# Another order of the statements on the four compute engines of a six-layer transformer pipeline

## The reference

```python
for i in range(DEPTH):                       # 6
    x = attn_layer(shift_tokens(x), Wqkv[i], q_scale[i], k_scale[i], Wo[i]) + x
    x = ffn_layer(shift_tokens(x), ln_g[i], ln_b[i], W1[i], b1[i], W2[i], b2[i]) + x
```

## Time and profile before

| | us |
|---|---|
| median of 3 runs | 3971.73 (3968.78 to 3972.18) |
| the profiled execution: its time | 3966.87 |
| its span | 3965.1 |
| PE busy | 3589.4 (91%) |
| PE's weight loads busy | 2946.9 (74%) |
| DVE busy | 3022.7 (76%) |
| ACT busy | 2842.0 (72%) |
| POOL busy | 2308.3 (58%) |
| share of PE in the chain that ended last | 67% |

### The profile page before, as it was taken

One profiled execution on the slowest core, in us unless ns is written; L12 is line 12 of the kernel. 1 busy time (PEld: TensorE's weight loads), 2 busy tenths in 40 slices (PEclk: granted clock), 3 DMA queues, 4 the chain that ended last, 5 costly groups with the idle time before them and its releaser, 6 DMA issues.

```text
span 3965.1 us, 140581 instructions
## 1 busy us (share of the span) xinstructions
PE 3589.4 (91%) x58802; PEld 2946.9 (74%) x58802; DVE 3022.7 (76%) x5808; ACT 2842.0 (72%) x5375; POOL 2308.3 (58%) x2139
## 2 busy tenths in 40 slices
PE   4755645999999999999999999999999999999998
PEld 3634433788878888878888888888788887888886
DVE  4577767877787777887777877777877778877774
ACT  2322214888888888888888888888888888878886
POOL 1000004767666667766677666776667766666762
PEclk9777756999999999999999999999999999999999
DMA  2000002433333333344333333333333333343332
GB/s 63 24 30 12 2 13 63 114 93 88 90 88 105 105 89 88 94 105 111 91 87 88 94 100 105 90 92 93 105 106 89 88 94 93 95 108 98 102 98 55
DMA packets 149461, 331.94 MB, mean 84 GB/s; under 512 B 17632, under 2 KB 27616, under 8 KB 147168
## 3 DMA queue, kind: packets, MB, share of 16 engines
q1 hardware_dynamic: 148832, 322.93, 30.7%
HBM read 218.01 MB, written 104.86 MB: 81 GB/s over the span
## 4 chain that ended last, share of the span: by engine, by line
PE 67%; DVE 7%; ACT 6%; issue 4%; POOL 0%; DVEq 0%; ACTq 0%; POOLq 0%
PE bank L1670 19%; PE bank L1729 9%; PE bank L1787 8%; PE bank L1760 7%; PE bank L1707 7%; PE bank L1744 4%; PE bank L1837 3%; PE bank L1775 3%; ACT L1328 3%; PE bank L1828 3%; DVE rot_a L1470 2%; DVE rot_b L1477 2%; DVE ss L1485 2%; ACT pT L1262 1%; ACT gate L1328 1%
## 5 line engine op out<-in xcount | busy, mean ns | idle before, releaser
L1131 POOL TENSOR_TENSOR qk<-rot_a,rot_b 128x512 f32<-128x512 f32 x768 | 985.8, 1284 | 763.0 <-PE bank L1707 746.4
L1141 POOL TENSOR_TENSOR qk<-qk,rn 128x512 f32<-128x512 f32 x768 | 798.9, 1046 | 144.2 <-DVE rn L1549 144.2
L1470 DVE TENSOR_TENSOR rot_a<-bank,rot 128x512 f32<-128x512 f32 x768 | 528.9, 689 | 265.3 <-PE bank L1670 256.9
L1213 ACT ACTIVATE sq<-bank 128x512 f32<-128x512 f32 x768 | 461.5, 601 | 223.1 <-DVE rot_b L1477 165.8
L1670 PE MATMUL bank<-w_hi,xs_hi 128*128 128x512 f32 x1152 | 583.1, 506 | 35.4 <-POOL xs_lo L1121 18.2
L1485 DVE TENSOR_REDUCE ss<-sq 128x8 f32<-128x512 f32 x768 | 515.6, 671 | 46.3 <-ACT sq L1213 46.1
L1477 DVE TENSOR_TENSOR rot_b<-bank,rot 128x512 f32<-128x512 f32 x768 | 522.1, 680 | 0.0
L1707 PE MATMUL bank<-ident,qk 128*128 128x128 f32 x3072 | 471.1, 276 | 4.7 <-ACT qT L1224 1.9
L1670 PE MATMUL bank<-w_lo,xs_hi 128*128 128x512 f32 x1152 | 458.2, 398 | 0.0
L1670 PE MATMUL bank<-w_hi,xs_lo 128*128 128x512 f32 x1152 | 456.6, 396 | 0.0
L1729 PEld LDWEIGHTS bank<-kT,qT 64*32 64x32 f32 x24576 | 359.9, 107 | 121.1 <-issue 120.9
(11 more groups left out here) (235 smaller groups left out, 6843.8 us busy)
## 6 DMA issues: line engine op xcount, KB each, us to landing
vw<-value_scratch SPq DMA_DIRECT2D x576, 256.0 KB, 4.9
value_scratch<-v SPq DMA_DIRECT2D x192, 512.0 KB, 2.7
vw<-value_scratch SPq DMA_DIRECT2D x192, 192.0 KB, 3.7
stage<-in_wqkv SPq DMA_DIRECT2D x6, 1536.0 KB, 9.3
stage<-in_wb_all SPq DMA_DIRECT2D x6, 1088.0 KB, 9.1
stage<-in_band SPq DMA_DIRECT2D x6, 512.0 KB, 4.9
d_xt<-in_x SPq DMA_DIRECT2D x4, 512.0 KB, 4.6
base_scratch<-d_res SPq DMA_DIRECT2D x4, 512.0 KB, 3.1
```

What stands on the lines that cost most here:

```text
L1131: nc.gpsimd.tensor_tensor(qk[:, c, :], rot_a[:, c % 2, :], rot_b[:, c % 2, :], ALU.add)\
L1141: nc.gpsimd.tensor_tensor(y, y, rn[:, x.q, 8 * c:8 * c + 8].unsqueeze(2).to_broadcast([P, 8, DH]), ALU.mult).then_inc(S["scaled"], 1)
L1213: nc.scalar.activation(sq[:, :], proj_bank(x, c)[:, :], ACT.Square).then_inc(S["squared"], 1)
L1470: nc.vector.tensor_tensor(rot_a[:, c % 2, :].rearrange("p (h d) -> p h d", h=8), proj_bank(x, c)[:, :].rearrange("p (h d) -> p h d", h=8), ...
```

## The change

The statements stay the same and their number too. Their order within `body` changes on POOL, ACT, DVE and PE; that of SP does not. On PE: `value(turn, 0)` and `turn_heads(out, 1)` stand ahead of `query_key(new, 0)`; `score(att, 2)` stands directly behind `score(att, 1)`; `turn_probs(out, 3)` and `weigh(out, 3)` come earlier; parts 1 and 0 of `ffn_in` come later, behind `value(turn, 1)`, and between them and part 2 now stand `turn_qk(turn, 2)`, `query_key(new, 3)` and `score(att, 3)`, where it was `turn_qk(turn, 1)`, `query_key(new, 2)` and `weigh(out, 3)`; `score(att, 3)` leaves its place behind `join_heads`. The other engines' lists are rearranged to go with it. The hunks are POOL, ACT (five), DVE (three) and PE (two); 16 columns of indentation are cut and lines of context that don't matter are left out.

```diff
@@ -1161,24 +1161,24 @@
 else:
     low_half(new, "prepared", NPREP)
 add(turn, 7)
+norm(out, 3)
 scale(turn, 0)
-norm(out, 3)
 scale(turn, 1)
 add(new, 0)
 scale(turn, 2)
 add(new, 1)
+scale(turn, 3)
 norm(att, 0)
-scale(turn, 3)
+add(new, 2)
 scale(turn, 4)
-add(new, 2)
 add(new, 3)
 scale(turn, 5)
+norm(att, 1)
 add(new, 4)
-norm(att, 1)
 scale(turn, 6)
+add(new, 5)
 norm(att, 2)
 scale(turn, 7)
-add(new, 5)
 add(new, 6)
@@ -1335,26 +1335,28 @@
 new, turn, att, out, ffn = b.items
+high_half(b, new)
+if b.switch == 1:
+    need(act, S["loaded_b"], b.layer * 16 + 16)
+    need(act, S["wo_done"], out.u)
+    nc.scalar.activation(wo[:, :, :].rearrange("p c n -> p (c n)"), stage_wo, ACT.Copy)\
+        .then_inc(S["conv_act"], 1)
 square_centred(ffn)
 if b.first and b.edge == -1:
...
     for c in (0, 2, 1, 3):
         convert(b.layer, c, "projected", 0)
-high_half(b, new)
-if b.switch == 1:
-    need(act, S["loaded_b"], b.layer * 16 + 16)
-    need(act, S["wo_done"], out.u)
-    nc.scalar.activation(wo[:, :, :].rearrange("p c n -> p (c n)"), stage_wo, ACT.Copy)\
-        .then_inc(S["conv_act"], 1)
+probs_out(out, 2)
+heads_taken(out, 1)
 square(turn, 7)
 if b.switch == -2 and not b.first:
     convert(b.layer, 3, "projected", turn.u * 8 + 8)
-probs_out(out, 2)
 exp(out, 3)
-heads_taken(out, 1)
+mask_scores(att, 1)
+mask_scores(att, 2)
+turned_out(att, 7)
 roots(turn, ffn)
-mask_scores(att, 1)
 value_out(turn, att, 0)
 square(new, 0)
...
 heads_out(out, 1)
 heads_taken(out, 2)
-turned_out(att, 7)
-exp(att, 0)
-affine(ffn)
-heads_out(out, 2)
-turned_out(turn, 0)
+probs_out(out, 3)
 square(new, 1)
...
-probs_out(out, 3)
-gelu(ffn)
-mask_scores(att, 2)
+turned_out(turn, 0)
+exp(att, 0)
+affine(ffn)
+heads_out(out, 2)
 turned_out(turn, 1)
 square(new, 2)
...
+mask_scores(att, 3)
+value_out(turn, att, 1)
+gelu(ffn)
+turned_out(turn, 2)
 heads_taken(out, 3)
-value_out(turn, att, 1)
-turned_out(turn, 2)
 square(new, 3)
 if b.first and b.edge == -2:
     for i in (6, 7):
@@ -1390,15 +1391,14 @@
     nc.scalar.preload_act_table_set(EXP_LN_TABLE)
 probs_out(att, 0)
 turned_out(turn, 3)
+heads_out(out, 3)
 exp(att, 1)
-heads_out(out, 3)
 square(new, 4)
...
 if b.next:
     convert(b.next, 0, "projected", new.u * 8 + 5)
-heads_taken(att, 0)
 value_out(turn, att, 2)
 if b.switch == -2:
     convert(b.layer, 4, "v_projected", turn.u * 4 + 3)
@@ -1406,20 +1406,23 @@
     need(act, S["y_done"], ffn.u + 1)
     nc.scalar.activation(w1[:, :, :, :].rearrange("p a c n -> p (a c n)"), stage_w1, ACT.Copy)\
         .then_inc(S["conv_act"], 1)
-mask_scores(att, 3)
+heads_taken(att, 0)
+turned_out(turn, 4)
 exp(att, 2)
-turned_out(turn, 4)
+mask_scores(turn, 0)
 square(new, 5)
...
 if b.next:
     convert(b.next, 2, "projected", new.u * 8 + 6)
-mask_scores(turn, 0)
 shift_state(out)
 probs_out(att, 1)
+heads_out(att, 0)
 turned_out(turn, 5)
-heads_out(att, 0)
+value_out(turn, att, 3)
+if b.switch == -2:
+    convert(b.layer, 5, "v_projected", turn.u * 4 + 4)
 square(new, 6)
 if b.first and b.edge == -2:
     for i in (11,):
@@ -1429,9 +1432,6 @@
         zero_values(i)
 if b.next:
     convert(b.next, 1, "projected", new.u * 8 + 7)
-value_out(turn, att, 3)
-if b.switch == -2:
-    convert(b.layer, 5, "v_projected", turn.u * 4 + 4)
 turned_out(turn, 6)
 nc.scalar.preload_act_table_set(EXP_LN_TABLE)
@@ -1589,6 +1589,7 @@
 new, turn, att, out, ffn = b.items
+total(out, 3)
 if b.first and b.edge == -2:
     for half in range(2):
         scale_rotation(b.layer, half, "rotated", 0)
@@ -1599,48 +1600,49 @@
 if b.switch == -1:
     convert(b.layer, 5, 6)
 polish(turn, ffn)
-total(out, 3)
+sum_squares(new, 0)
+rotate(new, 1, 0)
+rotate(new, 1, 1)
 deviate(ffn)
-rotate(new, 1, 0)
-sum_squares(new, 0)
-rotate(new, 1, 1)
-total(att, 0)
+top(att, 1)
 sum_squares(new, 1)
+shift(att, 1)
 rotate(new, 2, 0)
 rotate(new, 2, 1)
-top(att, 1)
-hidden(ffn)
+total(att, 0)
 sum_squares(new, 2)
 rotate(new, 3, 0)
 rotate(new, 3, 1)
 if b.next:
     scale_rotation(b.next, 0, "rotated", new.u * 16 + 8)
-shift(att, 1)
+hidden(ffn)
 top(att, 2)
 sum_squares(new, 3)
 rotate(new, 4, 0)
 rotate(new, 4, 1)
-shift(att, 2)
 layer_out(ffn)
 if b.switch == 1:
     need(dve, S["loaded_b"], b.layer * 16 + 16)
     need(dve, S["layer_out"], ffn.u + 1)
     nc.vector.tensor_copy(w2[:, :, :].rearrange("p c n -> p (c n)"), stage_w2).then_inc(S["conv_dve"], 1)
+shift(att, 2)
 total(att, 1)
 rotate(new, 5, 0)
-rotate(new, 5, 1)
 sum_squares(new, 4)
 if b.next:
     convert(b.next, 0, 1)
+rotate(new, 5, 1)
 total(att, 2)
 attended(out)
 out_add(b, ffn)
 top(att, 3)
 rotate(new, 6, 0)
-rotate(new, 6, 1)
 sum_squares(new, 5)
 if b.next:
     convert(b.next, 2, 2)
+rotate(new, 6, 1)
+top(turn, 0)
+shift(att, 3)
 centre(out)
 sum_squares(new, 6)
 if b.next:
@@ -1649,15 +1651,13 @@
 rotate(new, 7, 1)
 if b.next:
     scale_rotation(b.next, 1, "rotated", new.u * 16 + 16)
-top(turn, 0)
-shift(att, 3)
+shift(turn, 0)
+if b.switch == -2:
+    convert(b.layer, 4, 5)
 sum_squares(new, 7)
 if b.next:
     convert(b.next, 3, 4)
 floors(new, out)
-shift(turn, 0)
-if b.switch == -2:
-    convert(b.layer, 4, 5)
@@ -1854,29 +1854,30 @@
 turn_qk(att, 7)
 if b.first and b.edge == -1:
     pe.wait_ge(S["prepared"], NPREP)
-query_key(b, new, 0)
 value(b, turn, 0)
 turn_heads(out, 1)
+query_key(b, new, 0)
 weigh(out, 2)
 score(att, 1)
+score(att, 2)
+turn_probs(out, 3, turn, 0)
 query_key(b, new, 1)
 spread(ffn)
 turn_heads(out, 2)
 turn_qk(turn, 0)
-turn_probs(out, 3, turn, 0)
+weigh(out, 3)
+query_key(b, new, 2)
+turn_qk(turn, 1)
+value(b, turn, 1)
 ffn_in(ffn, 1)
 ffn_in(ffn, 0)
-turn_qk(turn, 1)
-query_key(b, new, 2)
-weigh(out, 3)
-ffn_in(ffn, 2)
-value(b, turn, 1)
 turn_qk(turn, 2)
 query_key(b, new, 3)
-score(att, 2)
+score(att, 3)
+ffn_in(ffn, 2)
+turn_qk(turn, 3)
 turn_probs(att, 0, turn, 1)
 turn_heads(out, 3)
-turn_qk(turn, 3)
 query_key(b, new, 4)
 ffn_out(ffn)
 value(b, turn, 2)
@@ -1885,20 +1886,19 @@
 query_key(b, new, 5)
 join_heads(b, out)
 turn_output(b, ffn, turn.u * 8 + 5)
-score(att, 3)
+turn_probs(att, 1, turn, 2)
+turn_heads(att, 0)
 query_key(b, new, 6)
-turn_probs(att, 1, turn, 2)
 turn_qk(turn, 5)
-turn_heads(att, 0)
-mean(out)
 value(b, turn, 3)
-turn_qk(turn, 6)
-query_key(b, new, 7)
 score(turn, 0)
 if b.switch == 1:
     need(pe, S["conv_act"], b.layer * 2 + 2)
     need(pe, S["conv_dve"], b.layer + 1)
+turn_qk(turn, 6)
+mean(out)
 turn_probs(att, 2, turn, 3)
+query_key(b, new, 7)
 weigh(att, 1)
 variance(out)
```

## The result

The changed kernel takes **4046.82 us** (median; 4041.51 to 4051.51), the kernel before 3971.55 beside it: ratio **1.019** (95%: 1.0178 to 1.0202), +75 us. The prediction said 3956, range 3930 to 3986.

What follows compares the result with a forecast made beforehand. TensorE, 98% busy in a steady stretch, was taken to bound the kernel. Its terms gave -0.12 us a body, -11 over 95; last layer -3, layer switches -4 and +2: -16 from 3971.73, so 3956 us, range 3930 to 3986.

Steps and rivals of the forecast that it cites:

- Shapes: TensorE's tile shape changes around `score` and `weigh`: six runs per body instead of seven, one entry and exit less, -0.20 us.
- Score behind score: Second of two adjacent scores on TensorE: between no gain and an exit's cost (0.11) saved; taken as -0.09 us a body.
- Third part: TensorE's wait on the GELU before `ffn_in`'s third part: 0.45 before, 0.40 remains (bounds 0.3 to 0.5), -0.05 us a body.
- First part: TensorE's wait at the first part of `ffn_in`, released by ScalarE's `affine`: the 0.10 goes, -0.10 us a body.
- value(turn, 3): New TensorE wait at this projection for the bank that `probs_out(att, 1)` empties: +0.25 us a body (0.15 to 0.35).
- turn_heads(out, 3): New TensorE wait at these transposes for the first of `hidden`'s three steps: between 0 and 0.11, taken as +0.07 us.
- the rivals: GELU wait vanishes, 3918 us, chance 0.10; nothing measurable, about 3974, chance 0.25; slower by the GELU chain, 3989, chance 0.13.
- Rival 3: Slower: the VectorE and ScalarE chain to the GELU loses its overlap, 0.35 us more at `ffn_in`'s third part; 3989, chance 0.13.
- a wait at `turn_qk`, `weigh` or `turn_probs`: Sign that the forecast is wrong: TensorE waiting at one of these statements, which was expected nowhere.

Runs made afterwards that it cites:

- e8_before_late: The kernel before, with each item's second window waiting on the SP queue until the item's third score has run: 3987.23 us, ratio 1.0038.
- e7_late: The changed kernel, with each item's second window waiting on the SP queue until the item's third score has run: 3954.78 us, ratio 0.9961.

## Why the prediction was wrong

The step that failed is the first sentence of its change part: "No instruction is added or taken away, no wait is dropped and no DMA is touched; (...) So I sum what each of TensorE's waits becomes." The same instructions came closer together, and their supply was priced at nothing, without a reason; it cost 78 us of pauses in 92 bodies, and the lower clock behind some of them. So was the SP queue: its reads were left out of the sum, but the run had become one that could not bear them (moving them took 92 us off). Term by term, in a quiet body:

- *Shapes*, -0.20: not measured apart.
- *Score behind score*, forecast -0.09 between 0 and -0.11: **-0.24** (1.82 against 2 x 1.03). The bound from the exit was too narrow. A likely reason is that the second score begins in the other half of the rows while the first still runs; no run tests it. The Trainium skill, "TensorEngine Tiling (Array Packing)", Key Properties, says that different tiles work in parallel; the 1.82 agrees.
- *Third part*, a wait of 0.40: 18.6 / 66 = 0.28. By the same view it was 27.3 / 72 = 0.38 before, not 0.45, so the term is -0.10. (The chain's terms add up to 5.61, not 5.63; that changes nothing.) First part: no wait, as forecast, -0.10. *`value(turn, 3)`*, +0.25: weight loads waited 0.26 each for `probs_out` in the changed kernel (the fence below this list). Right.
- *`turn_heads(out, 3)`*, +0.07: 0.06 (a step of 0.50 for 0.44 in the chain).
- Sum with the measured terms, and the shapes as forecast: -0.20 - 0.24 - 0.10 - 0.10 + 0.26 + 0.06 = -0.32; the quiet body shows -0.30, that is -28 us in 95 bodies. The order was better than forecast.

```profile
PEld bank L1670 <- ACT pT L1262: 18.8, 72, 0.3
```
Against that stand 70 us over the quiet length in 60 bodies (50 of them pauses), some 111 in 95: pauses and the clock behind them. -28 + 111 is 83, near the 75 measured. None of the rivals had it. Rival 3 was slower by another chain (the GELU's), which got shorter. The text named as a sign of error a wait at `turn_qk`, `weigh` or `turn_probs`; that is where part of the issue rows are (`weigh` has 23.7 us), but no reason was given for one.

The trace of before held what was needed: 470 instruction packets of 16,384 bytes, and in the earlier trace rows a `weigh` of 32 matmuls and a `score` of 64 in about 1 us each. It even held the price, in the mixer, which the change does not touch. Of the 42 blocks there that last less than 3.2 us, 41 are followed by a pause of 0.6 to 3.2 us, 55 us in all, each 1.2 to 1.6 us behind the end of a fetch. One line of these waits (0 to 720 us), and a stretch of them, with the DMA engines 2% busy and the clock at 0.55:
```profile
PE d_ps L829 <- issue: 12.7, 10, 1.5
```
```profile
160.00:190.00 30.00, 19.72 (x1089) 17.70 (x1090) 17.94 (x40) 2.77 (x4) 0.00 (x0) 0.55 0.02 5
```
So a dense run pauses without the window's transfers too. The Trainium skill, "Runtime: NRT & Kernel Launch", Instruction fetch mechanics, says that instructions come in blocks of 256, the next fetched while one is executed, and that crossing a boundary is mostly hidden. The first half agrees with the 470 packets. The second holds where a block of the changed kernel lasted over 6.5 us (0.1 us lost in 273 blocks) and fails in the dense run (pauses of up to 3.1 us), in the mixer, and behind the long blocks of `e8_before_late`.

## What to carry to other kernels

When statements are reordered, count instructions as well as time: in the changed kernel 41 of the 95 blocks of 256 instructions that TensorE used up in less than 5.5 us were followed by a pause over 0.5 us, and 2 of the 284 longer ones. If bodies of one loop differ in length and the waits say "issue", look for the period in instructions, and at what the DMA queues do at that moment. Then spread the dense statements, or move the transfers; in this kernel a pair of scores without a weigh beside it gave 0.9%.

## What the runs showed of the hardware

- A fetch of 16 KB took mostly 0.9 to 1.6 us in the changed kernel, and in its 48 pauses over 0.4 us after 720 us TensorE went on 1.15 to 1.7 us after its end. In the long body shown its start came about 2 us later than in `e7_late`, where the window's reads were moved.
- A pause of 3.07 us cost 6.2: the granted clock fell from 1.00 to 0.50 and was there for all of the 5 us shown. Behind pauses of 0.72 (above) and 1.19 us (below, in the changed kernel) it stayed at 1.00.
```profile
2246.08 1.19 issue
```
```profile
2247.40:2249.90 2.50, 2.50 (x21) 1.97 (x17) 1.23 (x4) 1.10 (x3) 0.98 (x2) 1.00 0.00 0
```
- The length of the pause does not decide it alone. In the changed kernel the clock stayed at 1.00 behind one of 2.50 us and was at 0.50 behind one of 1.97:
```profile
2280.61 2.50 issue
...
3474.98 1.97 issue
```
```profile
2283.10:2286.00 2.90, 2.88 (x44) 2.33 (x45) 0.36 (x2) 1.97 (x4) 1.86 (x2) 1.00 0.02 6
3477.10:3480.50 3.40, 3.40 (x38) 2.98 (x41) 2.21 (x4) 1.34 (x3) 1.23 (x2) 0.50 0.78 289
```
- What stays open: what sets the start of a fetch. That a boundary a few instructions earlier makes it start 1 to 3 us sooner was read off the table, not tested.
